# Splitting the expert weights in an attention phase: one set in three on GpSimd, clearing stores among the weight transfers, weights read in their plain layout

## The reference, cut to what matters

```python
x = x + xattn(layernorm(x), ctx)          # 32 batches, 64 tokens, 1601 context rows, width 512
x = x + attn(layernorm(x))                # 16 heads of 32, causal
# feed-forward, on h = layernorm(x):
probs = softmax(h @ w_router.T);  expert_weight, expert_idx = top_k(probs, 2)
inter = relu(einsum('ecd,efd->ecf', binned, w1_stack)) ** 2     # 8 experts, 512 x 512
outb  = einsum('ecf,edf->ecd', inter, w2_stack)
shared_out = (relu(h @ ws1.T) ** 2) @ ws2.T
```

## Time and profile before

| | |
|---|---|
| time, median of 3 runs | 1287.01 us (1286.15 to 1287.58) |
| profiled execution, its own time | 1287.01 us |
| its span, first to last instruction | 1285.3 us |
| PE busy | 1252.0 us, 97% of the span |
| DVE busy | 773.6 us, 60% |
| ACT busy | 365.5 us, 28% |
| POOL busy | 150.3 us, 12% |
| granted TensorE clock, mean | 0.998 of full speed |

### The profile page before, as it was taken

How to read it: one execution, slowest core, us unless ns; L and a number is a source line. 1 busy time by engine, 2 the same in 40 slices (tenths; PEclk the granted TensorE clock), 3 DMA queues, 4 the chain that set the end, 5 groups by cost and what they waited for, 6 DMA issues and landing times.

```text
span 1285.3 us, 21979 instructions
## 1 busy us (share of the span) xinstructions
PE 1252.0 (97%) x7654; PEld 844.5 (66%) x7655; DVE 773.6 (60%) x1414; ACT 365.5 (28%) x593; POOL 150.3 (12%) x154
## 2 busy tenths in 40 slices
PE   6999999999999999999999999999999999999998
PEld 3444444444444444467888888899998888888843
DVE  4456555655555544478988887757543555555556
ACT  2322212212121211235555544542222333233300
POOL 1000000000000000003000005501430000000054
PEclk9999999999999999999999999999999999999999
DMA  9999999999999999824768876731648545554587
GB/s 356 411 418 416 415 416 418 419 419 418 418 418 405 399 403 386 316 88 164 265 236 284 269 282 249 280 132 52 269 172 321 178 155 186 179 192 159 168 324 245
DMA packets 103763, 375.95 MB, mean 293 GB/s; under 512 B 10656, under 2 KB 33184, under 8 KB 88992
## 3 DMA queue, kind: packets, MB, share of 16 engines
q1 hardware_dynamic: 98592, 358.52, 73.1%
q0 software_dynamic: 5120, 16.78, 3.6%
HBM read 368.45 MB, written 69.73 MB: 341 GB/s over the span
## 4 chain that ended last, share of the span: by engine, by line
PE 90%; DVE 5%; DMA 1%; issue 1%; ACT 1%; SPq 1%; DVEq 0%; ACTq 0%
PE ps L1982 14%; PE ps L1870 13%; PE ps L2054 12%; PE ps L2044 10%; PE ps L2335 6%; PE ps L2338 6%; PE ps L2341 6%; PE ps L1945 4%; PE ps L1828 3%; PE ps L2402 2%; PE ps L2394 2%; PE ps L1960 2%; DMA arena<-ctx_n 1%; PE ps L1920 1%; PE ps L2073 1%
## 5 line engine op out<-in xcount | busy, mean ns | idle before, releaser
L1982 PE MATMUL ps<-arena 128*64 128x512 f32 (+1 forms) x832 | 192.5, 595 | 0.0
L2054 PE MATMUL ps<-split 128*128 128x256 f32 x1344 | 170.4, 285 | 10.3 <-DVE split L1325 10.0
L1870 PE MATMUL ps<-arena 128*64 128x512 f32 (+1 forms) x1024 | 177.3, 502 | 1.2 <-DVE arena L1266 0.7
L2054 PEld LDWEIGHTS ps<-split 128*128 128x128 f32 x1344 | 163.6, 191 | 15.1 <-issue 12.5
L1870 PEld LDWEIGHTS ps<-arena 128*64 128x64 f32 x1024 | 65.0, 137 | 121.0 <-issue 119.1
L1982 PEld LDWEIGHTS ps<-arena 128*64 128x64 f32 (+1 forms) x832 | 58.4, 137 | 112.7 <-issue 112.0
L1222 DVE SCALAR_TENSOR_TENSOR arena<-arena,hbar 128x512 f32<-128x512 f32 x128 | 90.5, 749 | 67.9 <-PE ps L1945 66.3
L760 ACT ACTIVATE arena<-ps 128x512 f32<-128x512 f32 (+1 forms) x93 | 52.2, 581 | 248.3 <-PE ps L1945 180.3
L2044 PE MATMUL ps<-split 128*128 128x512 f32 x384 | 96.7, 400 | 1.1 <-DVE arena L1393 1.1
L1196 DVE TENSOR_TENSOR F<-arena,ps 128x512 f32<-128x512 f32 x16 | 11.0, 687 | 135.9 <-ACT split L805 135.9
L2044 PEld LDWEIGHTS ps<-split 128*128 128x128 f32 x384 | 69.7, 188 | 17.7 <-issue 2.0
(11 more groups left out here) (228 smaller groups left out, 2001.4 us busy)
## 6 DMA issues: line engine op xcount, KB each, us to landing
arena<-ctx_t SPq DMA_DIRECT2D x122, 800.5 KB, 17.0
high<-parts_low SPq DMA_DIRECT2D x78, 1024.0 KB
arena<-ctx_n SPq DMA_DIRECT2D x96, 768.0 KB, 13.4
arena<-ctx_n SPq DMA_DIRECT2D x32, 1024.0 KB, 14.7
parts_high<-split SPq DMA_DIRECT2D x16, 1024.0 KB, 8.8
parts_low<-split SPq DMA_DIRECT2D x16, 1024.0 KB, 10.7
moe_in<-zero SPq DMA_DIRECT2D x3, 3328.0 KB, 17.6
moe_out<-arena SPq DMA_DIRECT2D x39, 256.0 KB, 2.1
```

Source lines behind the costliest of these rows:

```text
L1870: last = mm(bank(n)[S * h:S * (h + 1), 0:w], qT[:, k, S * h:S * (h + 1)], ctxT[h][:, k, at_j:at_j + w], start=(k == 0), stop=(k == KD - 1))
L1982: last = mm(bank(7)[S * h:S * (h + 1), :], ET[0:w, c, S * h:S * (h + 1)], ctxN[h][0:w, c, :], start=(c == 0), stop=(c == JC - 1))
L2054: last = mm(dst[:, 2 * P * m:2 * P * (m + 1)], w[a][:, k, c], tokens[b][:, k, :], start=(k + i == 0), stop=(k == KD - 1 and i == 2))
```

## The change

The diff does four things.

- The third low part of each stage (sets 2, 5, 8, 11 and 14) is computed on POOL, in one instruction of 128 x 2048, behind `add_bm` of the tiles 5, 7, 9, 11 and 13. POOL's loop over the tiles is written out. SP waits for these sets on a semaphore of their own, `low_pool`.
- The clearing of `moe_in` is cut into 13 stores of 3 slots (768 KB each) in place of 3 of 13 slots. Each is issued by SP right behind the low part's store of the sets 1 to 13.
- The raw matrices are read in their plain layout, 4 pieces of 2 KB for each partition, in place of one piece of 8 KB from an array that the host had laid out by partition. What lands in SBUF is the same.
- The router's weights `wr_sb` take the place of `zero`, so their load waits for all 13 clearing stores.

```diff
-ZEROED = 3
+ZEROED = 13
...
-        wr_sb = within("wr_sb", stage_at[-1][1] + KD * D + D, KD, P)
...
-        xgT = zero[:, :].rearrange("p (k n) -> p k n", n=P)
+        wr_sb = zero[:, :].rearrange("p (k n) -> p k n", n=P)
...
+        xgT = wr_sb
...
+            w_src = [w.rearrange("e (k p) n -> p e k n", p=P) for w in (w1t, w2t)]
+
             def load_raw(n):
-                sp.dma_start(stage_raw[n % NB].rearrange("p k n -> p (k n)"), (w1t, w2t)[n // E][n % E]
-                             ).then_inc(raw_in[n % NB], 16)
+                sp.dma_start(stage_raw[n % NB][:, :, :], w_src[n // E][:, n % E, :, :]).then_inc(raw_in[n % NB], 16)
...
                 store_part(n, parts_high, stage_high)
-                sp.wait_ge(low_done, n + 1)
+                if n % NB == 2:
+                    sp.wait_ge(low_pool, n // NB + 1)
+                else:
+                    sp.wait_ge(low_done, n + 1 - (n + 1) // NB)
                 store_part(n, parts_low, stage_low)
+                if 1 <= n <= ZEROED:
+                    if n == 1:
+                        sp.wait_ge(pool_filled, ZERO)
+                    zero_slots(n - 1)
+            sp.wait_ge(slots_zeroed, 16 * ZEROED)
             sp.dma_start(wr_sb[:, :, :], w_router.rearrange("(k p) n -> p k n", p=P)).then_inc(wr_in, 16)
             sp.wait_ge(parts_out, 32 * NS)
             sp.dma_start(raw_ws2[:, :, :], ws2t.rearrange("(k p) n -> p k n", p=P)).then_inc(ws_in, 16)
-            sp.wait_ge(pool_filled, ZERO)
-            zero_slots(0)
             sp.wait_ge(k_done, T)
             sp.wait_ge(ws_in, 16)
             sp.dma_start(raw_ws1[:, :, :], ws1t.rearrange("(k p) n -> p k n", p=P)).then_inc(ws_in, 16)
-            for q in range(1, ZEROED):
-                zero_slots(q)
...
-            with pool.Fori(0, T) as t:
+            def low_of_set(n):
+                i = n % NB
+                pool.wait_ge(high_done, n + 1)
+                nc.gpsimd.tensor_tensor(stage_low[i], stage_raw[i][:, :, :], stage_high[i].bitcast(F32), ALU.subtract
+                                        ).then_inc(low_pool, 1)
+
+            for t in range(T):
                 add_bm(t)
+                if t >= 5 and t % 2 == 1 and NB * ((t - 3) // 2) - 1 < NS:
+                    low_of_set(NB * ((t - 3) // 2) - 1)
...
                     residual_b(a - 2)
-                if last and more and NB * n < NS:
-                    low_of_set(NB * n - 1)
                 if now:
                     masked_scores(a, first)
```

More of the change, by code:

```diff
@@ L353, in perceiver_layer @@
         CONSTS, KBD0, VBD0, KBD1, VBD1, ZERO, IOTA = 9, 10, 13, 14, 17, 18, 22
-        raw_in, high_done, low_done, parts_out = (
-            [sem(f"raw_in{i}") for i in range(NB)], sem("high_done"), sem("low_done"), sem("parts_out"))
+        raw_in, high_done, low_done, low_pool, parts_out = (
+            [sem(f"raw_in{i}") for i in range(NB)], sem("high_done"), sem("low_done"), sem("low_pool"), sem("parts_out"))
         hold = sem("hold")
@@ L2419, in cols @@
         return np.asarray(v).reshape(KD, P).T
-    def by_rows(stack):
-        return np.asarray(stack).transpose(0, 2, 1).reshape(E, KD, P, D).transpose(0, 2, 1, 3).reshape(E, P, KD * D)
     ctx = np.asarray(ctx_1024)
@@ L2448 @@
         "w_router": w_r,
-        "w1t": by_rows(L0_ffn_w1_stack),
-        "w2t": by_rows(L0_ffn_w2_stack),
+        "w1t": np.asarray(L0_ffn_w1_stack).transpose(0, 2, 1),
+        "w2t": np.asarray(L0_ffn_w2_stack).transpose(0, 2, 1),
         "ws1t": np.asarray(L0_ffn_ws1).T,
```

## The result

The changed kernel took 1303.71 us (median of 4 runs, 1297.04 to 1306.6), against 1286.58 us for the kernel before in the same comparison: a ratio of 1.0127, 95% interval 1.0085 to 1.0168. It is slower, by 1.3%. I had forecast no change (1287.7 us, up to 1294.0).

A forecast was written before the change was run, and what follows sets the result against it. PE, busy 97% of the span, was taken as the bound, with DVE holding it up at one place in stages 1 to 5. 1287.0 + 0.5 (L1406 behind POOL) + 0.2 (set 14) + 0 = 1287.7 us; range 1284.3 to 1294.0.

The forecast's parts named there:

- Part 3: Thirteen clearing stores in the sets' transfer cycle: 1.92 us each, 0.5 us of it unhidden per cycle, bounds 0 and 1.92.
- the transfers become the bound: Rival in the sets' transfers: clearing or small pieces lengthen the cycle; 1294.6 us at +1.0, 1304 at +1.9; chance 0.24.
- the rival's own sum: Cost of a longer transfer cycle: 12 x added cycle - 5.9 + 0.5 us, giving +17 at +1.9.
- Set 15's spare of 5.9 us: Lateness allowed a set at a stage's end before PE feels it: ACT's 3.85 us idling plus 2.1 us.
- the table: Transfer cycle's cost, 12 x added cycle - 5.9 us, set against six kernels' measured losses; fits within 0.1 to 4.1 us.
- the pause is there to be filled: Argument against a transfer-bound slowdown: the transfers' pause at each load's start takes up some 1.4 us of clearing.
- Part 1: Third low part leaves DVE: 2.27 us less ahead of PE's wait for `h1_low`, at best -8.9 us.
- The bound of -8.9 us: Most that PE could win at its five waits for `h1_low`, 1.77 us of idling each.
- Part 2: Low part on POOL, 4.9 us (4.9 to 5.2 gives +0.5 to +2.0): DVE's L1406 waits for it, saving given back.
- Part 4: Raw loads in 2 KB pieces: -0.2 us per transfer cycle taken, from -0.8 to some tenths more.
- Part 5: The rest: clearing gone from behind the sets, router's weights' load waiting for clearing, POOL's written-out loop; 0 us each.
- a late set at 0.2 us: Set 14 rounded, and POOL started, 0.3 to 0.6 us late, which DVE's L1406 passes on once: +0.2 us.

The follow-up runs named there:

- e1_clear: Kernel before with only the clearing moved: 13 stores of 768 KB among the sets; 1310.26 us against 1288.47, ratio 1.0183.
- e9_two_slots: Kernel before with clearing stores of 512 KB in 13 rounds among the sets, the other 13 slots behind them; 1289.25 us against 1289.11, ratio 0.9999.
- e6_no_third: Kernel before without the third low part's subtraction, the high part stored in its place for five sets; 1281.09 us, ratio 0.9927.
- e3_pool: Kernel before with only the third low part of a stage moved to POOL, in one instruction; 1284.8 us, ratio 0.9979.
- e2_rows: Kernel before with only the raw matrices' loads changed to 2 KB pieces; 1288.5 us, ratio 1.0005.
- e11_mended: Changed kernel with POOL's low part in four instructions, 256 KB clearing per round, router's weights in their own place; 1281.32 us against 1289.11 for the kernel before.
- e8_twice: Kernel before with two 768 KB clearing stores behind each set's low part, the second to a spare array; 1301.8 us against 1290.67, ratio 1.0074.
- e10_between: Kernel before with the 768 KB clearing store issued between a round's load and its high part's store; 1302.53 us against 1289.11, ratio 1.0104.
- e14_held: Kernel before with 768 KB clearing per round and the next load held until the clearing landed; 1307.82 us against 1288.26, single run.
- e4_pool_rows: Kernel before with the third low part on POOL in one instruction plus 2 KB pieces for the raw loads; 1285.51 us, ratio 0.9978.

## Why the prediction was wrong, point by point

**The step that failed** is Part 3: "The pause takes up some 1.4 us of the 1.92, and 0.5 us stick out." Alone, the clearing added 1.99 us to a cycle (`e1_clear`), and with all parts in 1.69. The term lay at the bound I had given, 1.92. The price of the bytes was right and so was the length of the pause: 1.28 us of clearing do fit in (`e9_two_slots`), and of 1.92 us some 0.56 stick out, 0.5 by my sum. What was wrong is the price of what sticks out. I took it as 0.5 us of cycle for 0.5 us of transfer. In place of that, fifteen engines keep their pause and one clears through it, starts the next load some 2.4 us behind the end of its clearing, and so ends the round late; SP waits for the last of the sixteen.

**The rival and its range.** The mechanism of "the transfers become the bound" was right as I had put it: issues over 12.4 us apart, and a PE that waits for ACT. Its price at the bound, 1304 us, is what was measured, but in part by luck: a cycle grew by 1.69 us and not by 1.9, and with 1.69 the rival's own sum gives 12 x 1.69 - 5.9 + 0.5 = 14.9, 1301.9 us. The missing 1.8 us were not in my sum. Set 15's spare of 5.9 us fits the table to within its 4.1 us; no run tests it by itself. I gave the case 0.24 and cut the range at +1.0 us, though the rows did not tell 1.0 from 1.9: "the pause is there to be filled" was an argument about an average, and nothing in the trace of before showed a fourth transfer in that pause.

**Part 1** was right: DVE is the bound at that one place, and without the low part a stage falls to 31.07 us (`e6_no_third`; 31.1 forecast). The bound of -8.9 us came out as -7.0 over the six stages; one stage there took 33.5 us: ACT waited up to 6.8 us for a load in it, and PE 0.8 us for ACT's copies.

**Part 2** was right in kind. The hold also bites for an instruction of 4.6 us, so it isn't let go after 1.3 us, and the subtraction ends 1.08 us behind POOL. By the rule of the Trainium skill that the prediction named (SBUF — State Buffer, who interferes with whom), the trace agrees, now at 4.6 us. The term was mis-sized: 4.61 us measured, 4.9 taken, and POOL starts 0.08 us behind ACT in `e3_pool`, not 0.15. Five times the 0.36 us of both make -1.3 us of my +0.5, and `e3_pool` has -1.4. The fixed part of an instruction was taken from fills, which are another kind; 4 x 1.30 - 4.61 gives 0.2 us for each instruction saved. The Trainium skill's 4497 ns (GPSIMD Engine Reference, side-by-side cycle accounting) is nearer to the trace, 0.11 us short of it. With it, the forecast for this part would have been about -1.5 us, the low end of the range that I gave it and close to what the stages of `e3_pool` show.

**Part 4**, the 2 KB pieces, was right: nothing (`e2_rows`).

**Part 5** was not undone by a run of its own (`e11_mended` undoes it for the router's weights, together with other edits). No wait for the router's weights turned up among PE's waits.

**Not foreseen:** a late set moves POOL's start. In the late stages POOL starts 0.5 us ahead of the subtraction and not 2.5, so DVE stands 5.21 us at it. I had priced a late set at 0.2 us in the forecast and "about 1" in the rival.

**Still open:** why an engine that clears 0.56 us into the load joins it 2.4 us later; why twice the bytes cost less (13.26 us in `e8_twice`) than the same store once (13.84); and why the full change, with the same clearing, has a cycle 0.3 us shorter than the clearing alone.

## What to carry to other kernels

A store put into the pause of a chain of dependent transfers is free only while the slowest DMA engine is done with it before the next link's first bytes move (here about 1 us after its issue); past that size it may cost all of its duration in each link, so size it (here 512 KB) and look at the DMA share in the pause. Work moved to POOL should go in short instructions wherever DVE's next instructions read two inputs from SBUF: it is the length of one POOL instruction that DVE pays, not the sum. And where rows can't tell the middle of a term from its bound, the range has to reach the bound, with the number of times that the term counts.

## What the runs showed of the hardware that I had not expected

**A threshold.** In each cycle 256 KB and 512 KB of clearing added nothing (11.62 and 11.75 us against 11.85), 768 KB added 1.4 to 2.4 us on average in every arrangement, and 1536 KB 1.4 us. In `e10_between` and `e14_held` that is the clearing's own time in the chain; in the other three it is the late engine.

**PE's clock after a wait.** Windows of the changed kernel (us; PE's busy time second, the granted clock third from the end):

```profile
712.00:715.90 3.90, 0.77 (x17) 0.57 (x17) 1.53 (x2) 3.31 (x4) 0.00 (x0) 1.00 0.95 384
715.90:719.30 3.40, 3.40 (x29) 2.80 (x26) 3.37 (x8) 1.35 (x3) 0.00 (x0) 0.50 0.18 54
719.30:736.00 16.70, 13.69 (x120) 10.77 (x118) 14.15 (x17) 8.35 (x11) 7.38 (x3) 1.00 0.82 289
```

PE stood still for 3.13 us before `attend_b` started, and was busy for 0.77 us of 3.9. Then for 3.4 us the granted clock was 0.50, the lower of the two levels (1.2 in place of 2.4 GHz), with PE busy all the time. About half of those 3.4 us is lost, 1.7 us. There are four such stretches in phase B of the changed kernel and 17 us in all in that of `e1_clear`; near the start both have one more, as the kernel before has. Four times 1.7 is about the 6.1 us by which PE's busy time grew, and probably part of what the table's sum falls short by. So this wait of 3.13 us cost about half as much again. Shorter waits are not free of it: `e2_rows`, whose waits of PE from 600 to 820 us are 1.8 us at most, has three stretches of 3.4 us at 0.50 there.

**The scatter of the kernel before.** With a mean clock of 1.000 its runs took about 1286.1 us, at 0.995 to 0.996 1289.4 to 1291.3 (the 29 runs beside `e1_clear` to `e4_pool_rows`). `e3_pool` ran at 1.000 in 9 of 12 runs, the kernel before in 7 of 29. Among runs at 1.000 alone, `e3_pool` is 1.7 us faster (1284.4 against 1286.1), which is in line with its stages' 1.36 us; the rest of its 3.7 us in the medians goes with the clock.
